# Two stages of a sixteen-stage network on one core: expert tiles gathered by an inverted map, and a single-head attention reordered

## What is computed

```python
def _L2_attn_a_ref(x, WQ, WK, WV):
    q = jnp.einsum('bse,ke->bsk', x, WQ)
    k = jnp.einsum('bse,ke->bsk', x, WK)
    v = jnp.einsum('bse,ve->bsv', x, WV)
    scores = jnp.einsum('bsk,btk->bst', q, k) * SCALE
    masked = jnp.where(jnp.tril(scores) == 0, -jnp.inf, scores)
    attn = jax.nn.softmax(masked, axis=-1)
    return jnp.einsum('bst,btv->bsv', attn, v)
...
def _L2_ffn_ref(x, gate_w, gate_b, w1, b1, w2, b2):
    probs = jax.nn.softmax(xt @ gate_w + gate_b, axis=-1)
    _, idx = jax.lax.top_k(probs, TOP_K)                  # 2 of 8 experts
    mask = (one_hot.sum(axis=1) > 0).astype(xt.dtype)
    h1 = jax.nn.relu(jnp.einsum('th,ehf->etf', xt, w1) + b1[:, None, :])
    out_e = jnp.einsum('etf,efh->eth', h1, w2) + b2[:, None, :]
    out = jnp.einsum('eth,te->th', out_e, mask)
...
    x = x + _L2_attn_a_ref(_layernorm(x, axis=-1), ...)
    x = x + _L2_ffn_ref(_layernorm(x, axis=-1), ...)
    x = x + _L2_attn_b_ref(_layernorm(x, axis=-1), ...)
    x = x + _L2_ffn_ref(_layernorm(x, axis=-1), ...)
```

## Time and profile before

| | |
|---|---|
| runs | 2967.19, 2968.0, 2973.27 us; median 2968.0 us |
| profiled execution | 2966.24 us, its span 2964.7 us |
| TensorE busy | 2295.0 us, 77% of the span |
| VectorE, ScalarE, GpSimd busy | 1800.1, 1393.2, 858.3 us |
| granted TensorE clock over the span | 0.902 of full speed |

### The profile page before, as it was taken

How to read it: one execution, slowest core, us unless ns; L and a number is a source line. 1 busy time by engine, 2 the same in 40 slices (tenths; PEclk the granted TensorE clock), 3 DMA queues, 4 the chain that set the end, 5 groups by cost and what they waited for, 6 DMA issues and landing times. The chain is left out here.

```text
span 2964.7 us, 36677 instructions
## 1 busy us (share of the span) xinstructions
PE 2295.0 (77%) x12494; PEld 1086.6 (37%) x12494; DVE 1800.1 (61%) x3201; ACT 1393.2 (47%) x2324; POOL 858.3 (29%) x852
## 2 busy tenths in 40 slices
PE   6678879999757757777766787799997578577777
PEld 2222344544336226223222223445443452362232
DVE  5959565554525725885559595655455357259855
ACT  5535536555423434545455355366544234346454
POOL 3721151000224433651037211500001243336410
PEclk9998989999869878999989989999998687789999
DMA  3002000000021221000000020000000311210000
GB/s 140 0 18 67 10 1 9 1 1 1 1 96 52 71 96 36 0 0 1 9 8 0 27 60 7 1 9 1 1 1 1 99 60 59 96 36 0 1 2 14
DMA packets 58912, 80.91 MB, mean 27 GB/s; under 512 B 10784, under 2 KB 38944, under 8 KB 58464
## 3 DMA queue, kind: packets, MB, share of 16 engines
q1 hardware_dynamic: 49376, 63.81, 6.7%
q0 software_dynamic: 4992, 10.76, 1.1%
q10 hardware_dynamic: 4352, 3.94, 0.5%
HBM read 53.83 MB, written 26.08 MB: 27 GB/s over the span
## 5 line engine op out<-in xcount | busy, mean ns | idle before, releaser
L2227 ACT ACTIVATE L1b_pr<-ps,L1b_mneg 128x512 f32<-128x512 f32 x256 | 173.5, 682 | 191.3 <-DVE L1b_mneg L2268 191.3
L2266 DVE TENSOR_REDUCE L1b_m<-ps 128x2 f32<-128x1024 f32 x128 | 156.7, 1225 | 88.7 <-PE ps L2117 83.5
L96 ACT ACT_TABLE_LOAD x44 | 56.5, 1283 | 286.7 <-PEq L495 64.8
L1478 POOL TENSOR_TENSOR L0a_db<-L0a_du,L0a_bs 128x1024 f32<-128x1024 f32 x64 | 150.5, 2360 | 106.9 <-DVE L0a_du L1589 61.9
L1478 POOL TENSOR_TENSOR L3a_db<-L3a_du,L3a_bs 128x1024 f32<-128x1024 f32 x64 | 150.4, 2359 | 106.0 <-DVE L3a_du L1589 59.5
L1901 ACT ACTIVATE L0b_pt<-ps 128x1024 f32<-128x1024 f32 x128 | 125.6, 1022 | 97.3 <-PE ps L1801 97.2
L1989 DVE TENSOR_REDUCE L0b_mx<-ps 128x1 f32<-128x512 f32 x256 | 157.9, 682 | 20.3 <-PE ps L1788 17.7
L2292 DVE COPY L1b_prt<-ps 128x512 f32<-128x512 f32 x128 | 88.5, 691 | 126.4 <-PE ps L2130 126.1
L267 POOL CAST L1g_xc<-xn 128x512 bf16<-128x512 f32 x2 | 1.5, 731 | 558.5 <-DVE xn L142 558.5
L1606 DVE TENSOR_TENSOR_SCAN L3a_hs<-ps,L3a_db 128x1024 f32<-128x1024 f32 x64 | 146.0, 2282 | 5.3 <-ACT ps L1398 5.3
L1606 DVE TENSOR_TENSOR_SCAN L0a_hs<-ps,L0a_db 128x1024 f32<-128x1024 f32 x64 | 146.0, 2281 | 4.2 <-ACT ps L1398 4.2
(11 more groups left out here) (697 smaller groups left out, 5293.0 us busy)
## 6 DMA issues: line engine op xcount, KB each, us to landing
L2f_wall<-expert_dram SPq DMA_DIRECT2D x32, 256.0 KB, 5.6
L2g_wall<-expert_dram SPq DMA_DIRECT2D x32, 256.0 KB
weights<-w_dram SPq DMA_DIRECT2D x5, 941.5 KB, 14.1
L0b_qs<-stack_dram SPq DMA_DIRECT2D x32, 96.0 KB, 2.2
stack_dram<-L0b_cut SPq DMA_DIRECT2D x24, 128.0 KB, 2.1
L2b_qs<-stack_dram SPq DMA_DIRECT2D x32, 96.0 KB, 2.2
...
```

What stands on the lines that cost most here:

```text
L1478: pool.tensor_tensor(db[:, n % DEEP, :, :], du[:, b, :, :], bcast(bs[:, n % DEEP, :], 1, 2), ALU.mult).then_inc(input_ready, 1)
L2227: act.activation(pr[:, s % 2, h, :], g.ps[:, 2 * (s % 2) + h, :], ACT.Exp, bias=mneg[:, s % 2, h:h + 1], accum_out=total[:, u % 2, t, h:h ...
L2266: dve.tensor_reduce(m[:, s % 2, :], g.ps[:, 2 * (s % 2):2 * (s % 2) + 2, :], AX.X, ALU.max).then_inc(max_raw, 1)
```

## The change

In `expert_ffn` the first scatter is gone. SyncE stores the tokens to a DRAM tensor `tokens`, each twice, so that row i holds the token of pair i (4 DMAs of 256 KB). VectorE builds, from the slots, two 0/1 tables, the tile (`of_tile`) and the place in the tile (`of_lane`) of each pair; 16 small bf16 matmuls multiply them with the pairs' numbers, so that a 128 x 23 map comes out that names the pair of every slot (`source`). GpSimd then gathers each tile straight from `tokens` by one indirect DMA, 23 in all: six ahead, then tile n+6 behind the scatter of tile n. TensorE turns single tiles, two ahead of use, and ScalarE copies each one (`x_copy`) behind the choice of its weights. The targets of the rows (`row`) come from the same map, once for all tiles.

In `single_head_attention` the scale is put into ScalarE's copy of q, and k is copied by VectorE. The mask is two VectorE operations that both read the scores in PSUM: the first marks zeros and later keys, the second adds -1e30 where marked. Three buffers of scores and of probabilities are used; VectorE does the first four operations of block n+1 ahead of the last two of block n; TensorE makes scores three blocks ahead and the product with v one block behind; the second batch's blocks run from wide to narrow.

The diff, cut to its core; `prepare` also loses the one DMA that filled `slots`, and `_pack` gets four small tables.

```diff
-GROUP = 4
+AHEAD = 6
...
-    sp.wait_ge(sent, 16 * 2 * NT)
-    for k in range(groups):
-        a, z = GROUP * k * P, (GROUP * k + size(k)) * P
-        sp.dma_start(xg[:, GROUP * k:GROUP * k + size(k), :], g.slots[a:z, :].rearrange("(t p) w -> p t w", p=P)).then_inc(group_in[k], 16)
+    for b in range(NB):
+        sp.wait_ge(tok_in, b + 1)
+        for k in range(2):
+            rows = g.tokens[2 * b * T:2 * (b + 1) * T, :].rearrange("(t p k) c -> p t k c", p=P, k=2)
+            sp.dma_start(rows[:, :, k, :], tok[:, b * KT:(b + 1) * KT, :]).then_inc(stored[b], 16)
...
+    for c in range(4):
+        pe.wait_ge(lanes_ready, c + 1)
+        for r in range(4 * c, 4 * c + 4):
+            mm = pe.matmul(g.ps[:, 0, 0:2 * SLOTS], of_lane[:, r, :], ids_of[:, r, :, :].rearrange("p k n -> p (k n)"),
+                           start=(r == 0), stop=(r == 2 * NT - 1))
+    mm.then_inc(named, 1)
...
-    def turn(k):
-        pe.wait_ge(group_in[k], 16)
-        if k >= 2:
-            pe.wait_ge(x_in, k - 1)
...
+    def turn(n):
+        pe.wait_ge(gathered[n % AHEAD], 16 * (n // AHEAD + 1))
+        if n >= 2:
+            pe.wait_ge(x_in, n - 1)
+        pe.transpose(g.ps[:, 4 + n % 2, 0:P], xg[:, n, :], g.w("ident")).then_inc(x_turned, 1)
...
     turn(0)
+    turn(1)
     hidden_products(0)
     for n in range(SLOTS):
-        if n % GROUP == 0 and n // GROUP + 1 < groups:
-            turn(n // GROUP + 1)
+        if n + 2 < SLOTS:
+            turn(n + 2)
         if n + 1 < SLOTS:
             hidden_products(n + 1)
         results(n)
...
-        act.wait_ge(cleared, 1)
-        for k in range(2):
-            act.activation(tok[:, k, b * KT:(b + 1) * KT, 0:P], g.ps[:, 6 + b, :].rearrange("p (t c) -> p t c", c=P), ACT.Copy).then_inc(tok_in, 1)
+        act.activation(tok[:, b * KT:(b + 1) * KT, :], g.ps[:, 6 + b, :].rearrange("p (t c) -> p t c", c=P), ACT.Copy).then_inc(tok_in, 1)
...
     choose(0)
+    x_copy(0)
     choose(1)
-    x_copy(0)
...
+    x_copy(1)
+    for n in range(2, SLOTS):
+        choose(n)
+        x_copy(n)
...
-    dve.tensor_scalar(slot[:, :], slot_f[:, :], -1.0, None, ALU.add).then_inc(slots_ready, 1)
+    dve.tensor_tensor(reached[:, :, :], bcast(slot_f[:, :], 2, SLOTS + 1), bcast(g.w("e2_step"), 1, 2 * NT), ALU.is_gt).then_inc(slots_ready, 1)
+    dve.wait_ge(slots_ready, 1)
+    dve.tensor_reduce(tile_f[:, :], reached[:, :, 1:SLOTS], AX.X, ALU.add).then_inc(slots_ready, 1)
+    dve.tensor_tensor(of_tile[:, :, :], reached[:, :, 0:SLOTS], reached[:, :, 1:SLOTS + 1], ALU.subtract).then_inc(slots_ready, 1)
+    dve.wait_ge(slots_ready, 2)
+    dve.scalar_tensor_tensor(out=lane[:, :], in0=tile_f[:, :], scalar=-float(P), in1=slot_f[:, :], op0=ALU.mult, op1=ALU.add).then_inc(slots_ready, 1)
+    dve.wait_ge(slots_ready, 3)
+    dve.tensor_tensor(ids_of[:, :, 0, :], of_tile[:, :, :], bcast(g.w("e2_low"), 2, SLOTS), ALU.mult).then_inc(slots_ready, 1)
+    dve.tensor_tensor(ids_of[:, :, 1, :], of_tile[:, :, :], bcast(g.w("e2_high"), 2, SLOTS), ALU.mult).then_inc(slots_ready, 1)
+    dve.wait_ge(slots_ready, 6)
+    for c in range(4):
+        dve.tensor_tensor(of_lane[:, 4 * c:4 * c + 4, :], bcast(lane[:, 4 * c:4 * c + 4], 2, P), bcast(g.w("e2_lane"), 1, 4), ALU.is_equal).then_inc(lanes_ready, 1)
...
+    dve.wait_ge(named, 1)
+    dve.tensor_copy(id_f[:, :], names[:, 0, :]).then_inc(ids_ready, 1)
+    dve.wait_ge(ids_ready, 1)
+    dve.scalar_tensor_tensor(out=id_f[:, :], in0=names[:, 1, :], scalar=float(2 * P), in1=id_f[:, :], op0=ALU.mult, op1=ALU.add).then_inc(ids_ready, 1)
+    dve.wait_ge(ids_ready, 2)
+    dve.tensor_copy(source[:, :], id_f[:, :]).then_inc(source_ready, 1)
...
-    def rows_of(k):
-        a, z = GROUP * k, GROUP * k + size(k)
-        dve.wait_ge(group_in[k], 16)
-        dve.tensor_tensor(row_f[:, a:z], xg[:, a:z, P], valid[:, a:z], ALU.mult).then_inc(rows_step, 1)
-        dve.wait_ge(rows_step, k + 1)
-        dve.tensor_tensor(row[:, a:z], row_f[:, a:z], spare[:, a:z], ALU.add).then_inc(rows_ready, 1)
+    dve.tensor_tensor(row[:, :], id_f[:, :], spare[:, :], ALU.add).then_inc(rows_ready, 1)
...
-    pool.wait_ge(slots_ready, 1)
-    for b in range(NB):
-        pool.wait_ge(tok_in, 2 * b + 2)
-        for t in range(b * KT, (b + 1) * KT):
-            for k in range(2):
-                pool.indirect_dma_start(g.slots[:, :], bass.IndirectOffsetOnAxis(ap=slot[:, k * NT + t:k * NT + t + 1], axis=0),
-                                        tok[:, k, t, :], None).then_inc(sent, 16)
+    pool.tensor_copy(wall[:, :, 2 * FF:SET], g.w("e2_b1").rearrange("p (e f) -> p e f", f=FT)).then_inc(bias_in, 1)
+    def gather(n):
+        pool.indirect_dma_start(xg[:, n, :], None, g.tokens[:, :],
+                                bass.IndirectOffsetOnAxis(ap=source[:, n:n + 1], axis=0)).then_inc(gathered[n % AHEAD], 16)
+    pool.wait_ge(source_ready, 1)
+    for b in range(NB):
+        pool.wait_ge(stored[b], 32)
+    for n in range(AHEAD):
+        gather(n)
+    pool.wait_ge(rows_ready, 1)
     for n in range(SLOTS):
-        pool.wait_ge(rows_ready, n // GROUP + 1)
         pool.wait_ge(y_in, n + 1)
         pool.indirect_dma_start(g.rows[:, :], bass.IndirectOffsetOnAxis(ap=row[:, n:n + 1], axis=0),
                                 y[:, n, :], None).then_inc(returned, 16)
-    pool.wait_ge(sent, 16 * 2 * NT)
+        if n + AHEAD < SLOTS:
+            gather(n + AHEAD)
...
+blocks = [(0, t) for t in range(KT)] + [(1, t) for t in reversed(range(KT))]
+width = lambda n: (blocks[n][1] + 1) * P
...
+q_bank, k_bank, v_bank, score_bank = (4, 2), (5, 3), (6, 7), (0, 1, 4)
...
-        b, t = n // KT, n % KT
-        if n >= 2:
-            pe.wait_ge(scaled, n - 1)
-        pe.matmul(g.ps[:, n % 2, 0:(t + 1) * P], q[:, b, t * P:(t + 1) * P], k[:, b, 0:(t + 1) * P],
+        b, t = blocks[n]
+        pe.wait_ge(q_in, b + 1)
+        pe.wait_ge(k_in, b + 1)
+        if n >= 3:
+            pe.wait_ge(masked, n - 2)
+        pe.matmul(g.ps[:, score_bank[n % 3], 0:width(n)], q[:, b, t * P:(t + 1) * P], k[:, b, 0:width(n)],
...
+    for n in range(3):
+        scores(n)
+    for n in range(N):
+        turns(n)
+        if n + 3 < N:
+            scores(n + 3)
+        if n >= 1:
+            values(n - 1)
+    values(N - 1)
...
+        act.wait_ge(proj, 3 * b + 1)
+        act.activation(q[:, b, :], g.ps[:, q_bank[b], :], ACT.Copy, scale=scale).then_inc(q_in, 1)
...
+    probs(0)
+    for n in range(N):
+        if n + 1 < N:
+            probs(n + 1)
+        take_turned(n)
...
+    def maxima(n):
+        w = width(n)
         dve.wait_ge(score, n + 1)
-        if n >= 2:
-            dve.wait_ge(prob, n - 1)
-        dve.tensor_scalar(s[:, n % 2, 0:w], g.ps[:, n % 2, 0:w], scale, None, ALU.mult).then_inc(scaled, 1)
-        dve.wait_ge(scaled, n + 1)
-        dve.tensor_tensor(s[:, n % 2, w - P:w], s[:, n % 2, w - P:w], g.w("tri"), ALU.mult).then_inc(mask_steps, 1)
-        dve.wait_ge(mask_steps, 3 * n + 1)
-        dve.tensor_scalar(zero[:, n % 2, 0:w], s[:, n % 2, 0:w], 0.0, None, ALU.is_equal).then_inc(mask_steps, 1)
-        dve.wait_ge(mask_steps, 3 * n + 2)
-        dve.scalar_tensor_tensor(out=s[:, n % 2, 0:w], in0=zero[:, n % 2, 0:w], scalar=NEG, in1=s[:, n % 2, 0:w],
-                                 op0=ALU.mult, op1=ALU.add).then_inc(mask_steps, 1)
-        dve.wait_ge(mask_steps, 3 * n + 3)
-        dve.tensor_reduce(m[:, n:n + 1], s[:, n % 2, 0:w], AX.X, ALU.max).then_inc(max_ready, 1)
-        dve.wait_ge(max_ready, 2 * n + 1)
-        dve.tensor_scalar(m[:, n:n + 1], m[:, n:n + 1], -1.0, None, ALU.mult).then_inc(max_ready, 1)
+        dve.scalar_tensor_tensor(out=none[:, n % 2, 0:w], in0=g.ps[:, score_bank[n % 3], 0:w], scalar=0.0, in1=later[:, T - w:T],
+                                 op0=ALU.is_equal, op1=ALU.max).then_inc(found, 1)
+        dve.wait_ge(found, n + 1)
+        if n >= 3:
+            dve.wait_ge(prob, n - 2)
+        dve.scalar_tensor_tensor(out=s[:, n % 3, 0:w], in0=none[:, n % 2, 0:w], scalar=NEG, in1=g.ps[:, score_bank[n % 3], 0:w],
+                                 op0=ALU.mult, op1=ALU.add).then_inc(masked, 1)
+        dve.wait_ge(masked, n + 1)
+        dve.tensor_reduce(m[:, n:n + 1], s[:, n % 3, 0:w], AX.X, ALU.max).then_inc(max_ready, 1)
+        dve.wait_ge(max_ready, n + 1)
+        dve.tensor_scalar(neg[:, n:n + 1], m[:, n:n + 1], -1.0, None, ALU.mult).then_inc(neg_ready, 1)
+    def norms(n):
+        w = width(n)
         dve.wait_ge(prob, n + 1)
         dve.reciprocal(inv[:, n:n + 1], total[:, n:n + 1]).then_inc(inverse, 1)
         dve.wait_ge(inverse, n + 1)
-        dve.tensor_scalar(pr[:, n % 2, 0:w], pr[:, n % 2, 0:w], inv[:, n:n + 1], None, ALU.mult).then_inc(norm, 1)
-    for b in range(NB):
-        dve.wait_ge(out_ready, (b + 1) * KT)
-        dve.tensor_tensor(g.xs[:, b, :], g.xs[:, b, :], g.ps[:, 4 + b, :], ALU.add).then_inc(added, 1)
```

(21 more changed lines are left out.)

184 lines of the change are left out of this document (86 added, 98 removed).

## The result

In the timed comparison the changed kernel takes 2924.22 us (median of 4 runs, 2922.69 to 2927.95) against 2970.64 (4 runs): ratio 0.9847, 95% interval 0.9832 to 0.9863. It is faster by 46 us, 1.5%, where the sum had 80 (52 + 28), and 0.2 us outside the range. The profiled execution took 2925.72 us, span 2924.1 against 2964.7.

A forecast was written before the change was run, and what follows sets the result against it. No engine bound either stage throughout: attention was VectorE and TensorE taking turns; experts mostly GpSimd before the first transpose, then TensorE. 2966.2 - 52 - 28 = 2886, stated as 2888 us for the median; range 2862 to 2924.

The forecast's parts named there:

- Attention, 52 us: Two attention stages: VectorE's work shortened and no longer taking turns with TensorE, 25.9 us saved a stage (24.4 to 27.3).
- Experts, up to the first tile: Expert stages: map replaces 16 scatters, then gather and landing; first transpose at 867.3 instead of 882.4, 15.1 us earlier.
- The estimate from the Trainium skill's fit: Gather's landing: about 2.0 us plus bytes at 436 GB/s, 2.15 from issue, so 1.2 behind GpSimd's part; sum 3 us lower.
- Rivals 1 to 3: Expert gathers: dearer than a scatter (0.03 slower, 0.10 about 2920), cheaper (2854 to 2875, 0.12), or not overlapping (2947, 0.03).
- The Trainium skill's rule to coalesce small transfers: Expert loads: under 64 KB one pays mostly overhead; six 288 KB loads became 23 of 64 KB, favouring dearer or non-overlapping gathers.
- One hidden term: Expert stages: token stores queue behind expert weights, ready at 1085.6 against the map at 1086.5, hidden by 0.9 us.
- Experts, the tiles: Expert tile loop: GpSimd becomes the bound, last scatter at 925.6 instead of 932.7; 7.1 us saved a stage, 28 for four.
- pair: Expert tile loop: one gather and one scatter on GpSimd, 2.52 us, for 17 tiles, where TensorE needs 1.91.
- the ring: Expert tile loop: result through scatter, gather n+6 and TensorE back, about 8.5 us against four tiles of 2.52; adds nothing.
- The sign that the prediction gives: Expert tile loop: if scatters start more than 1.26 us after a gather, the ring binds, not GpSimd.
- rival 1: Expert gathers cost GpSimd more than scatters: 2982 at twice a scatter, chance 0.03 slower; about 2920 for 1.45 to 2.3, 0.10.
- rival 4: Attention gains less, through TensorE's low clock or an overlooked wait: with half of the 52 us, 2914; chance 0.07.

The follow-up runs named there:

- fourth set: Runs on one chip at one time: the changed kernel again, unaltered, 2883.97 us, beside repeats of variants; the kernel before read 2969.2 to 2971.2 in these sets.
- e2: Changed kernel with all 23 gathers issued ahead of the first scatter: 2946.31 us; the same file again (e2_again) in the fourth set 2864.98 us.
- the first and the fifth set: Groups of variant runs, each on one chip beside the kernel before; the fifth reran the changed kernel, 2927.01 us; the first did not include it.
- second, third and fourth: Groups of runs, each on one chip; the unaltered changed kernel ran only in the last of these, 2883.97 us.
- e6: Changed kernel with the 17 gathers between the scatters replaced by plain loads of 128 rows that SyncE issues (output differs): 2853.28 us.
- e10: Changed kernel with the 17 gathers between the scatters replaced by plain loads that GpSimd issues (output differs): 2847.08 us.
- e1: Kernel before with only the new attention, expert layer untouched: 2907.31 us, ratio 0.9789; again in the fifth set 2908.1 us.
- e5: Changed kernel without the 17 gathers between the scatters, tile n reading the input of tile n mod 6 (output differs): 2847.7 us.
- e7: Changed kernel with the 17 gathers between the scatters replaced by second scatters of the same result to a spare tensor (output differs): 2870.54 us.
- e9: Changed kernel with its 17 gathers kept, but nothing waits for or reads what they bring (output differs): 2873.15 us.
- e12: Changed kernel with gathers and TensorE's waits kept, but tile n reads the input of tile n mod 6 (output differs): 2886.3 us, repeated 2884.54.
- e13: Changed kernel with all gathers ahead and SyncE relaying TensorE's waits for them: 2864.01 us, repeated 2860.8.

## Why the prediction was wrong, and where it was right

**Attention, 52 us: right in kind, 7.5 too small.** The durations are as priced: they add up to 18.6 us for 18.8. The first block starts at 790.12 (790.9 forecast); VectorE then runs to 808.65, 18.5 us where the sum has 20.4, since neighbours overlap in the trace, so that it is busy for 17.32 us, and the waits between them take 1.2 us where 1.6 was priced. From there to the end of the last addition it is 1.95 us; I had 3.3 in the sum, the middle between TensorE's low and high clock, and it is the high one (0.56 to 0.59 in the halves before, 0.91 now). Together the last addition ends at 810.6 and not 814.6. The stage came to 31.5 us where the text expects about 35.

**Experts, up to the first tile: right.** Map 6.2 us behind the slots (6.9 forecast), first transpose 9.4 (10.5), gather 0.95 + 0.30. Its landing, up to the transpose, is 1.69 us behind GpSimd's part in the comparison and 1.55 in the fourth set (1.8 taken). The estimate from the Trainium skill's fit, page "DMA: Bandwidth & Descriptors", "Anatomy of one DMA", was 1.2, shorter than either; by the prediction's own steps it would have made the sum nearer 5 us lower than 3, since tile 22 meets the landing a second time. Rivals 1 to 3, all on the gather's price or overlap, are out: in e2 the first two transposes come 1.23 us apart (836.15, 837.38), although a gather lands 2.5 us or more after its issue. The Trainium skill's rule to coalesce small transfers (same page, "Rules for kernel authors") would have made the 64 KB transfers the cost, and the trace does not bear that out: the pair took GpSimd's 2.57 us in the fourth set. One hidden term showed once: in the fourth set's first `L2g` GpSimd's first gather waits for the stores of the tokens and starts 1.74 us behind the map, where it is 0.80 in `L2f`; the prediction had them hidden by 0.9 us.

**Experts, the tiles: this step failed in the comparison.** The prediction has "pair" 2.52 us with GpSimd as the bound, "so it adds nothing" of the ring and ScalarE "under 2.52". Where signals are on time it is so: 2.57 us a pair, 51.9 us for 22 tiles (50.3 forecast), and the four stages save 29.5 us for 28. In the comparison the pair took 3.00 us and the 22 tiles 60.7, because signals of TensorE came up to 4 us late through the whole of the loop, and 7.1 saved a stage became 1.6 lost. The sign that the prediction gives, scatters that start more than 1.26 us after a gather, was there (848.98 to 851.68, 2.70 us): the ring did bind, with 3 us in it that are no engine's work. No rival held this. The nearest in number, the dearer gather of rival 1 at about 2920, has the wrong cause, as the gather took the 0.95 + 0.30 us forecast; rival 4 puts the loss in the attention, and its 2914 is 10 us short.

**The total.** In the comparison's two traces the span falls by 40.6 us: 59.5 in the attention, less 6.3 in the experts, less 12.6 in the rest. Against the forecast of 80 that is 7.5 more, 34 less and 12.6 less. So a second term failed, smaller than the ring: the rest, for which the sum has nothing; why it grows stays open. Where signals are on time the measured 2883.97 lies near the 2888 forecast, but partly by luck: 9 us too little gained in the two kinds of stage by the sum, against 7.3 us that the rest gave back. The range was built from prices of instructions alone; a bound for a wait that grows for an outside reason was not in it.

**What stays open.** Signals were late in the comparison, the first and the fifth set, and on time in the second, third and fourth. The number that each set's record gives its chip does not sort them (the first and third have the same, with opposite results), though it may not name the same silicon. Within a set it did not change: the four executions of the comparison agree within 0.2%, those of the fourth set within 0.4%.

One thing in the traces does sort the sets, whatever the kernel: in the late sets records of raised semaphores are missing. Of ScalarE's signals in the tile loops 6 to 71 are missing in each trace of the late sets, none in the others. Of the 1472 steps by which the scatters of the results report their landing, the trace of the comparison holds 664 and that of the fourth set all (the traces of e6 and e10, on time too, 1421 and 1411). Steps are missing also where no time is lost in a late set: 1075 are left in the kernel before, 1147 and 1131 in e1, 1062 in e5. In the view of DMA issues the landing's time (the last number) is then missing; the comparison and the fourth set:

```profile
rows<-L2f_y,L2f_row POOLq DMA_INDIRECT x46
...
rows<-L2f_y,L2f_row POOLq DMA_INDIRECT x46, 2.3
```

So the condition of the late sets is there in the kernel before too, which does not feel it. Whether it delays the signals and the records alike, or whether the recording itself takes part in the delay, no run separates.

Shown: it is TensorE's signals that are late, not VectorE's or ScalarE's; in late sets a kernel has them with the 17 gathers in the loop or ahead of it (up to 3.9 us, and 22 us in e2, with the gathers closest together), and next to none without (at most 0.4 us in e5, none in e1 and the kernel before); neither relaying the wait nor ScalarE's order helps. Not shown: that it must be gathers. Second scatters, plain loads or unread gathers might make signals late too, since e6, e7, e9, e10 and e12 never ran in a late set; and what in the chip holds a signal back.

**A version that beats both**: e2 with e13, all gathers ahead. GpSimd runs 46 operations without a hole, the last scatter of the first stage starts at 892.00 in e2_again, and the experts take 356.4 us: 2861 to 2865 us, 19 to 23 below the changed kernel. But the same file takes 2946 in a late set, where e1 keeps its 2908. Which is better depends on how often a chip is in that condition, which six sets can't tell.
